# Routed experts: gate and up with the inner units on the partitions

## The reference

```python
xs = x * sigmoid(top_val)                       # x: layer-normed tokens, top expert of 8 per token
g = jnp.einsum('th,ehi->eti', xs, rt_gate)      # h = 128, i = 256
u = jnp.einsum('th,ehi->eti', xs, rt_up)
act = jax.nn.silu(g) * u
y = jnp.einsum('eti,eih->eth', act, rt_down)
routed = jnp.einsum('eth,te->th', y, onehot)    # only the token's own expert counts
```

## Time and profile before

| | us |
|---|---|
| median of 3 runs (1032.65 to 1035.71) | 1034.25 |
| profiled execution, its own time | 1042.43 |
| its span, first to last instruction | 1040.7 |
| TensorE busy (matmul) | 739.7 (71%) |
| TensorE weight loads | 502.4 (48%) |
| VectorE busy | 710.3 (68%) |
| ScalarE busy | 346.7 (33%) |
| GpSimd busy | 414.6 (40%) |
| routed stage `_m1`, first transpose to last scatter's start | 557.5 to 607.2 |
| routed stage `_m2`, the same | 979.7 to 1028.1 |

### The profile page before, as it was taken

One profiled execution on the slowest core, in us unless ns is written; L12 is line 12 of the kernel. 1 busy time (PEld: TensorE's weight loads), 2 busy tenths in 40 slices (PEclk: granted clock), 3 DMA queues, 4 the chain that ended last, 5 costly groups with the idle time before them and its releaser, 6 DMA issues. The chain is left out here.

```text
span 1040.7 us, 15374 instructions
## 1 busy us (share of the span) xinstructions
PE 739.7 (71%) x5487; PEld 502.4 (48%) x5487; DVE 710.3 (68%) x1213; ACT 346.7 (33%) x591; POOL 414.6 (40%) x597
## 2 busy tenths in 40 slices
PE   0566897777779995476577925488887778467694
PEld 0345455776679984254544613233333333254462
DVE  8997778999958885998342337678887786054132
ACT  0211381110015500122112514066766666411152
POOL 4344304888859601344151532223223332115053
PEclk9987899999969998688587967589999999868797
DMA  8000000000000003100012126484000000001213
GB/s 190 10 1 1 1 1 1 1 1 1 1 1 2 1 1 92 45 1 0 1 37 71 41 76 203 107 125 68 9 7 9 8 8 8 7 0 34 70 37 106
DMA packets 43024, 35.98 MB, mean 35 GB/s; under 512 B 6182, under 2 KB 37478, under 8 KB 42950
## 3 DMA queue, kind: packets, MB, share of 16 engines
q1 hardware_dynamic: 40390, 29.68, 12.2%
q0 software_dynamic: 2560, 5.31, 1.5%
HBM read 17.51 MB, written 15.89 MB: 32 GB/s over the span
## 5 line engine op out<-in xcount | busy, mean ns | idle before, releaser
L1990 DVE TENSOR_REDUCE blockmax<-c_bank 128x8 f32<-128x1024 f32 x144 | 174.9, 1223 | 47.5 <-PE c_bank L2116 41.3
L2053 ACT ACTIVATE PT<-c_bank 128x1024 f32<-128x1024 f32 x144 | 145.4, 1025 | 71.4 <-PE c_bank L2138 71.3
L2152 PE MATMUL c_bank<-PT,V 128*9 128x256 f32 (+3 forms) x960 | 78.6, 431 | 14.5 <-POOL PT L1942 10.4
L897 PE MATMUL sums<-prod,ident 128*128 128x128 f32 x512 | 68.2, 290 | 26.6 <-DVE prod L929 26.6
L2109 PE MATMUL c_bank<-KA,QA 48*128 48x128 bf16 (+3 forms) x608 | 59.9, 282 | 36.1 <-DMA KA<-qk_parts_dram 16.3
L1942 POOL TENSOR_SCALAR_AFFINE_SELECT PT<-PT 128x256 f32<-128x256 f32 x128 | 49.0, 406 | 80.8 <-ACT PT L2053 80.8
L897 PEld LDWEIGHTS sums<-prod,ident 128*128 128x128 f32 x512 | 62.7, 200 | 31.9 <-DVE prod L929 31.7
L1648 POOL DMA_INDIRECT routed_results<-results_m,rows_m x48 | 45.9, 957 | 78.0 <-DVE results_m L1625 74.9
L2138 PE MATMUL c_bank<-QA,KA 51*128 51x128 bf16 (+3 forms) x480 | 56.9, 302 | 16.7 <-DMA QA<-nrows 16.1
L1631 DVE TENSOR_TENSOR r_h_m<-r_silu_m,r_gu_m 128x256 f32<-128x256 f32 x48 | 20.2, 421 | 67.1 <-ACT r_silu_m L1616 67.1
L379 PE MATMUL gu_f<-gu_wT,xqT_f 128*128 128x352 f32 x128 | 52.9, 568 | 16.9 <-DVE h_f L307 16.9
(11 more groups left out here) (337 smaller groups left out, 1818.6 us busy)
## 6 DMA issues: line engine op xcount, KB each, us to landing
sorted_rows<-blank SPq DMA_DIRECT2D x2, 1584.0 KB, 12.2
rows_m<-sorted_rows SPq DMA_DIRECT2D x12, 264.0 KB, 4.4
qk_parts_dram<-qk_parts SPq DMA_DIRECT2D x8, 384.0 KB, 3.4
QA<-qk_parts_dram SPq DMA_DIRECT2D x6, 384.0 KB, 7.4
KA<-qk_parts_dram SPq DMA_DIRECT2D x6, 384.0 KB, 9.2
back_m<-routed_results SPq DMA_DIRECT2D x8, 256.0 KB, 3.8
qk_parts_dram<-qk_parts SPq DMA_DIRECT2D x8, 256.0 KB, 3.4
m_gu<-in_rt_gate SPq DMA_DIRECT2D x1, 1024.0 KB, 5.6
```

The source lines that it names most:

```text
L897: ins = nc.tensor.matmul(sums[:, kind, 0], k.ident[:, :], prod[:, kind, e // HALF, :, e % HALF, :], start=(e == 0), stop=(e == DH - 1))
L1990: nc.vector.tensor_reduce(blockmax[:, h % 2, :, HALFQ * n:HALFQ * (n + 1)], slot_of((1, m)).rearrange("p b (n c) -> p b n c", c=P), AX.X, ...
L2053: nc.scalar.activation(PT[:, u % PRING, :, :], slot_of((0, u)), ACT.Exp, scale=SCALE).then_inc(s_pt, 1)
L2152: ins = nc.tensor.matmul(O[32 * g:32 * g + DH + 1, f * P:f * P + n], V[:, b, j, h, :], PT[:, u % PRING, b, o:o + n], start=(j == 0), stop= ...
```

## The change

Gate and up change operands. The expert's weights are now stationary and the transposed rows move, so the product has the inner units on the partitions, as `down` wants them. It takes four products of 128 columns (two halves of gate, two of up) in place of one of 512. The expert's 512 columns are copied by ScalarE from `moe.gu` into a fixed buffer `expert` with two halves, by slot; the register address is then in ScalarE's copy, with a register load on ScalarE's queue three slots ahead, and no longer in TensorE's gate_up. `turn_h`, `hidden_columns`, `tph`, `h` and their semaphores go; VectorE writes `hT` directly and waits for `down` of two slots before. TensorE keeps its own register load for `down`.

```diff
-                    nc.tensor.matmul(gu[:, j % 2, :], rowsT[:, j % 2, :], moe.gu[:, bass.ds(owner[j], 1), :],
-                                     start=True, stop=True).then_inc(s_gu, 1)
-
-                def turn_h(j):
+                    pe.wait_ge(s_expert, j + 1)
+                    for n in range(2 * HALVES):
+                        ins = nc.tensor.matmul(gu[:, j % 2, n * P:(n + 1) * P], expert[:, j % 2, n * P:(n + 1) * P],
+                                               rowsT[:, j % 2, :], start=True, stop=True)
+                    ins.then_inc(s_gu, 1)
+
+                def down(j, e):
                     pe.wait_ge(s_h, j + 1)
-                    if j >= 2:
-                        pe.wait_ge(s_hT, j - 1)
-                    for t in range(HALVES):
-                        ins = nc.tensor.transpose(tph[:, j % 2, t * P:(t + 1) * P], h[:, j % 2, t * P:(t + 1) * P], k.ident[:, :])
-                    ins.then_inc(s_th, 1)
-
-                def down(j, e):
-                    pe.wait_ge(s_hT, j + 1)
...
                     if j >= 1:
                         down(j - 1, owner.pop(j - 1))
-                    turn_h(j)
...
-                def hidden_columns(j):
-                    act.wait_ge(s_th, j + 1)
-                    if j >= 2:
-                        act.wait_ge(s_y, j - 1)
-                    nc.scalar.copy(hT[:, j % 2, :], tph[:, j % 2, 0:INNER]).then_inc(s_hT, 1)
-
+                def expert_of(j):
+                    return act.value_load(which[0:1, j:j + 1], min_val=0, max_val=EXPERTS - 1)
+
+                def expert_weights(j, e):
+                    wait(act, s_gu, j - 1)
+                    nc.scalar.copy(expert[:, j % 2, :], moe.gu[:, bass.ds(e, 1), :]).then_inc(s_expert, 1)
+
+                owner = {j: expert_of(j) for j in range(3)}
+                for j in range(2):
+                    expert_weights(j, owner.pop(j))
                 columns(0)
                 columns(1)
                 for j in range(SLOTS):
+                    if j + 3 < SLOTS:
+                        owner[j + 3] = expert_of(j + 3)
                     act.wait_ge(s_gu, j + 1)
                     if j >= 2:
                         act.wait_ge(s_h, j - 1)
                     nc.scalar.activation(silu[:, j % 2, :], gu[:, j % 2, 0:INNER], ACT.Silu).then_inc(s_silu, 1)
                     if j + 2 < SLOTS:
                         columns(j + 2)
-                    hidden_columns(j)
+                        expert_weights(j + 2, owner.pop(j + 2))
...
                     if j >= 2:
-                        dve.wait_ge(s_th, j - 1)
-                    nc.vector.tensor_tensor(h[:, j % 2, :], silu[:, j % 2, :], gu[:, j % 2, INNER:2 * INNER], ALU.mult).then_inc(s_h, 1)
+                        dve.wait_ge(s_y, j - 1)
+                    nc.vector.tensor_tensor(hT[:, j % 2, :], silu[:, j % 2, :], gu[:, j % 2, INNER:2 * INNER], ALU.mult).then_inc(s_h, 1)
```

More of the change, by code:

```diff
@@ L1520, in moe_routed @@
         silu = k.sb(f"r_silu{tag}", [P, 2, INNER], ctx=ctx)
-        h = k.sb(f"r_h{tag}", [P, 2, INNER], ctx=ctx)
         hT = k.sb(f"r_hT{tag}", [P, 2, INNER], ctx=ctx)
+        expert = k.sb(f"r_expert{tag}", [P, 2, 2 * INNER], ctx=ctx)
+        s_expert = k.sem(f"s_expert{tag}")
         results = k.sb(f"results{tag}", [P, SLOTS, D], ctx=ctx)
@@ L1526, in moe_routed @@
         gu = k.ps(f"r_gu{tag}", [P, 2, BANK], ctx=ctx)
-        tph = k.ps(f"r_tph{tag}", [P, 2, BANK], ctx=ctx)
         y = k.ps(f"r_y{tag}", [P, 2, BANK], ctx=ctx)
-        names = ("s_added", "s_tx", "s_xT", "s_rgu", "s_rsilu", "s_rh", "s_th", "s_hT", "s_ry", "s_rres", "s_stored", "s_out")
-        s_added, s_tx, s_xT, s_gu, s_silu, s_h, s_th, s_hT, s_y, s_res, s_stored, s_out = (k.sem(f"{n}{tag}") for n in names)
+        names = ("s_added", "s_tx", "s_xT", "s_rgu", "s_rsilu", "s_rh", "s_ry", "s_rres", "s_stored", "s_out")
+        s_added, s_tx, s_xT, s_gu, s_silu, s_h, s_y, s_res, s_stored, s_out = (k.sem(f"{n}{tag}") for n in names)
         s_back = [k.sem(f"s_back{n}{tag}") for n in range(4)]
```

## The result

| | us |
|---|---|
| before, median of 4 runs (1032.65 to 1037.08) | 1034.98 |
| after, median of 4 runs (1054.81 to 1063.33) | 1059.59 |
| ratio, 95% interval | 1.0232 [1.0188, 1.0276] |
| profiled execution after, its own time and span | 1054.81, 1053.1 |

The change made the kernel 24.6 us slower; 22 were forecast. The two profiled executions lie only 12.4 us apart. The rest of the program, which the change doesn't touch, took 10.0 us less in the one after (mean granted clock over the span 0.882, before 0.868): 1053.1 - 61.5 - 61.8 = 929.8 against 1040.7 - 51.2 - 49.7 = 939.8. So I compare the routed stages, from TensorE's first register load to the start of the last scatter. The first grew from 51.2 (556.0 to 607.2) to 61.5 us (550.1 to 611.60), the second from 49.7 (978.4 to 1028.14) to 61.8 (979.0 to 1040.81).

A forecast was written before the change was run, and what follows sets the result against it. TensorE's own work bounded the routed stages; a TensorE-ScalarE ring would replace it. Per stage +11.5 us up to gate_up(23), start included, and -0.7 at the end, twice, made +22 on 1034.25: 1056 us, 8-in-10 range 1048 to 1078.

The forecast's parts named there:

- The ring: Warm routed slots: gate and up, transpose, ScalarE's small copy and expert copy follow one another, 2.14 us against 1.70.
- release of TensorE: Ring's last link, from the expert copy's end to the next gate_up: 0.07 us, bounds 0.04 and 0.14.
- TensorE's own work: TensorE's work in a warm routed slot: 1.49 us against 1.70, the saving lying inside its wait.
- Hidden work: ScalarE's register load and silu, down, VectorE's product and POOL's scatters fit inside the ring: no cost, down bound 0.15.
- Start: Start of each routed stage: ScalarE's three register loads and two expert copies precede columns(0), +1.4 us.
- Cold part: Half-clock slots of each routed stage: ring 3.16 us, cold part ending one slot later than today.
- End: End of each routed stage: last scatter 5.2 us after gate_up(23) against 5.96, 0.7 us sooner, set by POOL.
- The sum: Both routed stages: 2 x (11.5 - 0.7) = +21.6 us, giving a median of 1056 us.
- A dear copy: Rival 1, ScalarE's expert copy: 1.07 us for 0.61, or a costly register address; 1076 us, chance 0.12.
- The half clock: Rival 2, routed stages: waits keep TensorE's clock at half, 1095 us if it never rises; chance 0.13, whole or part.
- The faster case: Rival 3, routed slots: expert copy runs during gate_up, ahead of columns; ring 1.54 us, 1029 us, chance 0.04.
- No difference: Rival 4, routed slots: ring of 1.70 us, the expert copy costing 0.17; 1036 us, chance 0.03.

The follow-up runs named there:

- early_turn: Changed kernel with to_columns(j+2) ahead of gate_up(j+1) in TensorE's list: 1041.97 us, ratio to before 1.0027.
- expert_first: Changed kernel with expert_weights(j+2) ahead of columns(j+2) in ScalarE's list: 1040.47 us, ratio to before 1.0023.
- fixed_more: fixed_expert with 40 more waits a slot on gate_up's semaphore for idle SyncE: 1069.9 us (one run), period 1.80 us.
- both_lean: Changed kernel with early_turn's and expert_first's orders, shorter starts on ScalarE and TensorE, and register loads without bounds: 1038.27 us, ratio to before 0.9985.
- fixed_expert: early_turn with slot j always taking expert j % 8, so without register loads and register addresses: 1010.77 us, ratio to before 0.9822.
- first_lean: expert_first with a shorter start of ScalarE and register loads on both queues without bounds: 1033.92 us, ratio to before 0.9957.

## Why the prediction was right

**The ring (right, 3% small).** Link by link, forecast and measured in the slot above: gate and up to the transpose 0.99, 1.00; to columns 0.31, 0.31; to the expert copy 0.16, 0.16; the copy 0.61, 0.62; release of TensorE 0.07, 0.11 (end of the copy before, 1006.29 + 0.62, to 1007.02). The sum is 2.20 for 2.14. The mis-sized term is the release: I took a value in the middle of 0.04 and 0.14, since the wait of before had a register instruction behind it; the new one has none and still costs 0.11, so the row with the same direction was the one to take. Gate_up(0) to gate_up(23) therefore took 2.1 us more in the two stages together than forecast.

**TensorE's own work (right).** 1.49 forecast; early_turn's undisturbed slots give 1.45, with the eight passes at 0.90 (1007.45 to 1008.35) and down at 0.44. Against the section "Back-to-back issue gap" of the Trainium skill's "TensorE: Matmul & The Clock Gate", by which I had worked out a ring of 2.5, eight small fp32 passes cost what two long ones had.

**Hidden work (right).** After register load and silu ScalarE is still idle for 1.09 us before columns, down ends 0.4 us before the next gate_up, VectorE and POOL wait.

**Start (too dear).** gate_up(0) comes 3.0 us after the first load (979.0 to 981.99) and 3.2 in the first stage (550.1 to 553.30), against 2.1 and 2.4 before: +0.9 and +0.8 for +1.4. From ScalarE's first load to its first copy it is 1.7 us (978.9 to 980.64), I had 1.95, and from columns to gate_up 0.31, I had 0.41; in the first stage the start of before was 2.4 and not the 2.1 that I took for both.

**Cold part (right).** gate_up(0) to (1) 2.64 (forecast 2.73), then 3.26 and 3.23 (3.16; the same release again); the clock rose in the same slot as forecast in the second stage, one sooner in the first. gate_up(0) to gate_up(23): 53.2 and 53.7 for 52.4.

**End (right).** 5.11 us from gate_up(23) to the last scatter in both stages, 5.2 forecast, 5.96 before.

**The sum (closer than its terms).** The routed stages grew by 22.4 us for 21.6 forecast. In that, errors offset each other: +2.1 from gate_up(0) to gate_up(23), -1.1 at the starts, -0.2 at the ends. That this came out at 0.8 is luck in part. The rest of the 3.6 us between 1056 and the median of 1059.59 lies outside these stages: 0.7 is the median of before, which is 1034.98 with its fourth run, and the other 2.1 are less than the runs of the changed kernel differ among themselves (1054.81 to 1063.33).

**The rivals.** A dear copy falls: 0.62. The half clock falls: the granted clock stays at 1.00 with TensorE idle for some 0.45 us of each 2.20 (busy for 34.40 of 43.00). The Trainium skill, "TensorE: Matmul & The Clock Gate", section "HAM oscillation — how this bites in real kernels", has the clock sent back by waits that are longer than the bursts of products between them; here they are shorter, so this trace doesn't test it. The faster case had the right price list and the wrong order: expert_first is that case, 1.62 a slot where I wrote 1.54, since the passes still start from a standstill. No difference would have needed a copy of 0.17.

## What to carry to other kernels

Count an operand's copy not by its engine's load but by its place: ScalarE was busy for half the time, and yet 0.21 us less of copy was 0.21 less on the slot. When two engines hand work back and forth, walk once round the ring in program order, and put what waits for nothing ahead of what waits for the other engine; a buffer more doesn't do it. When a ring is opened and the period doesn't fall as worked out, look for releases that arrive long after their instruction's end before inventing a new dependency.

## What the hardware showed that I had not expected

Releases can come 1.8 us after the end of the instruction that sends them, while the sender runs on, and then several at once (early_turn, fixed_more, both_lean: mostly every third slot, some 5.5 us apart; expert_first: 7 slots of 48). An idle engine's waits sufficed to bring them on where scatters ran in the loop (fixed_more), and no kernel without scatters in the loop had them. It cost early_turn 0.4 us a slot, 1.85 for 1.45. What sets them off isn't known: they came at undisturbed slots of 1.45 and of 1.62 us, and in fixed_expert (1.45) and first_lean (1.62) they didn't. A period worked out from the ring alone is therefore a lower bound in a loop like this, and has to be measured.
